# Three attention layers in one kernel: the first layer's step plan re-ordered, and the cross layer's softmax denominators taken from one sum per pair of heads

## The reference, cut to what matters

```python
# first layer (L0): 20 heads of 8, two softmaxes on one set of queries
out = softmax(q k_text^T) v_text + softmax(q k_ip^T) v_ip      # 77 text keys, 435 ip keys
x = x + out @ Wo.T + bo
# a1: self-attention, 20 heads of 64, on n = layer_norm(x)
x = x + attention(n, n)
# a2: cross-attention, 20 heads of 64, keys and values from the context (512 keys)
x = x + attention(layer_norm(x), context)
x = x + feed_forward(layer_norm(x))
```

## Time and profile before

| | |
|---|---|
| median of 3 runs | 1611.23 us (1607.58 to 1615.48) |
| the profiled execution | 1616.8 us, of it 1615.0 us span |
| PE busy | 1536.3 us, 95% |
| VectorE / ScalarE / GpSimd busy | 64% / 48% / 29% |
| chain that ended last | PE 80%, VectorE 7%, ScalarE 6%, issue 6% |
| mean granted TensorE clock | 0.967 of full |

### The profile page before, as it was taken

The page is one execution under the profiler, slowest core; times in us unless marked ns, Lnnn a source line. Parts: engine busy times, 40 slices in busy tenths (PEclk is TensorE's granted clock), DMA queues, the critical chain, the costliest instruction groups (busy, mean ns, idle before and its releaser), DMA issues.

```text
span 1615.0 us, 41102 instructions
## 1 busy us (share of the span) xinstructions
PE 1536.3 (95%) x18128; PEld 1208.6 (75%) x18128; DVE 1028.1 (64%) x1410; ACT 776.1 (48%) x1061; POOL 465.9 (29%) x414
## 2 busy tenths in 40 slices
PE   7999999878999999999899999999999999999988
PEld 5566666546888887888778878888787878777788
DVE  6777777763776776766556555565655555565466
ACT  3666666654444454455344444444444444443323
POOL 4332333220222232334322332232322332232300
PEclk7989999968999999999999999999999999999999
DMA  5322232100000100000110000000000020000000
GB/s 149 94 58 59 58 132 63 43 1 22 2 2 2 58 35 2 6 2 18 37 48 2 2 28 2 28 2 28 2 28 2 1 71 2 1 2 2 2 13 21
DMA packets 26780, 45.54 MB, mean 28 GB/s; under 512 B 7344, under 2 KB 15472, under 8 KB 26224
## 3 DMA queue, kind: packets, MB, share of 16 engines
q1 hardware_dynamic: 26608, 42.96, 8.8%
HBM read 29.51 MB, written 1.31 MB: 19 GB/s over the span
## 4 chain that ended last, share of the span: by engine, by line
PE 80%; DVE 7%; ACT 6%; issue 6%; DMA 1%; POOL 0%; SPq 0%; ACTq 0%; POOLq 0%; DVEq 0%
PE a_pj L949 7%; PE a_pj L961 7%; PE l_px L1530 5%; PE a_pv L983 5%; PE a_px L983 4%; PE a_pj L495 4%; PE l_pscore L1453 3%; PE a_px L536 3%; PE a_pst L914 3%; PE a_pscore L893 3%; PE a_pv L522 3%; PE l_pst L1468 2%; PE a_px L999 2%; PE a_pj L504 2%; PE a_pst L920 2%
## 5 line engine op out<-in xcount | busy, mean ns | idle before, releaser
L1204 POOL TENSOR_TENSOR a_key_sum<-a_probs 128x512 f32<-128x512 f32 x160 | 209.4, 1313 | 449.4 <-ACT a_probs L1052 449.4
L1131 DVE TENSOR_REDUCE a_negmax<-a_pscore 128x2 f32<-128x1024 f32 x160 | 195.6, 1222 | 105.0 <-PE a_pscore L893 104.6
L1052 ACT ACTIVATE a_probs<-a_pst 128x1024 f32<-128x1024 f32 x160 | 164.1, 1026 | 168.3 <-PE a_pst L920 167.7
L1762 DVE TENSOR_REDUCE l_negmax<-l_pscore 128x2 f32<-128x154 f32 x320 | 203.5, 685 | 48.3 <-PE l_pscore L1453 47.6
L1647 ACT ACTIVATE l_probs<-l_pst 128x1024 f32<-128x1024 f32 x160 | 164.0, 1025 | 98.6 <-PE l_pst L1468 98.3
L736 POOL TENSOR_TENSOR a_key_sum<-a_probs 128x1024 f32<-128x1024 f32 x40 | 96.3, 2408 | 246.4 <-ACT a_probs L582 246.4
L655 DVE TENSOR_REDUCE a_negmax<-a_pscore 128x4 f32<-128x1024 f32 x80 | 97.6, 1220 | 54.4 <-PE a_pscore L453 54.3
L1145 DVE RECIPROCAL a_recip<-a_pv 128x256 f32<-128x256 f32 x40 | 70.3, 1757 | 88.9 <-PE a_pv L989 88.9
L961 PE MATMUL a_pj<-a_wv_hi,a_ct 128*128 128x256 f32 x640 | 111.2, 285 | 0.0
L582 ACT ACTIVATE a_probs<-a_pst 128x1024 f32<-128x1024 f32 x80 | 81.9, 1024 | 40.2 <-PE a_pst L479 36.3
L914 PE MATMUL a_pst<-a_qh,a_kh 64*128 64x256 f32 x640 | 96.7, 293 | 2.5 <-ACT a_probs L1052 1.5
(11 more groups left out here) (219 smaller groups left out, 3504.0 us busy)
## 6 DMA issues: line engine op xcount, KB each, us to landing
l_ct<-in_ctx_t SPq DMA_DIRECT2D x8, 512.0 KB, 4.3
l_k_stack<-l_k_hi SPq DMA_DIRECT2D x64, 64.0 KB, 2.1
a_ct<-in_ctx_t SPq DMA_DIRECT2D x8, 512.0 KB, 4.6
a_ct<-in_ctx_t SPq DMA_DIRECT2D x16, 256.0 KB, 5.1
l_q_stack<-l_q_hi SPq DMA_DIRECT2D x80, 32.0 KB, 1.9
l_x<-in_x_t SPq DMA_DIRECT2D x8, 256.0 KB, 4.2
l_k_stack<-l_k_lo SPq DMA_DIRECT2D x32, 64.0 KB, 2.1
a_raw_wq<-in_a_wq SPq DMA_DIRECT2D x2, 960.0 KB, 4.6
```

What stands on the lines that cost most here:

```text
L1052: nc.scalar.activation(probs[:, 2 * i:2 * i + 2, 2 * n:2 * n + 2, :], pst[:].rearrange("p h (k q) -> p h k q", k=2), ACT.Exp, scale=SCALE) ...
L1131: nc.vector.tensor_reduce(to, pscore[:], AX.X, ALU.max, negate=True).then_inc(max_done, 1)
L1204: nc.gpsimd.tensor_tensor(key_sums[n][:, two], probs[:, two, 2 * n, :], probs[:, two, 2 * n + 1, :], ALU.add).then_inc(sum_ready, 1)
L1762: last = nc.vector.tensor_reduce(to[:, :, k], pscores[s % 2][:, :, keys], AX.X, ALU.max, negate=True)
```

## The change

1. **Cross layer**: POOL makes three of the four additions; DVE adds, behind its fourth maximum of the step, the sums of heads 0-1, then the last pair of key tiles of heads 2-3, then the sums of heads 2-3, and only then the low keys. PE multiplies one sum instead of two.
2. **First layer, plan**: "out" moves from part 3 into part 1 of u = 2 and into another PSUM bank (`pj`, written by place 0 as well), with DVE adding it in part 1; the first value projection moves from u = 3 to u = 2, and the others up by one place. `norm` moves from step 37 to 35.
3. **First layer, start**: the marks are loaded ahead of the context; DVE writes those of buffer 0 before it takes the low keys and those of buffer 1 later; DVE, not POOL, rounds stack 0; PE waits for one value tile, ahead of its second score.
4. **Opening of a1**: it starts 3 steps earlier, in step 30, and its copies stand one by one between the parts of a step, `wv` in three pieces in step 36. The split weights lie in tensors of their own (`SplitMatrix`), and each is loaded by two DMAs.
5. All SBUF addresses (`AT`) are new.

```diff
-    PLAN = {0: ("ip", "text"), 1: ("q", "rest"), 2: (None, None), 3: ("v0", "v1"), 4: ("v2", "v3")}
+    PLAN = {0: ("ip", "text"), 1: ("q", "rest"), 2: (None, "v0"), 3: ("v1", "v2"), 4: ("v3", None)}
...
-        if t == ALL - 3:
+        if t == ALL - 5:
             return ("norm", place)
         b, u = divmod(t, GROUPS)
+        if u == 2 and place == 0 and 0 <= b - 2 < B - 1:
+            return ("out", b - 2)
...
-        OPEN, LOAD, FF_OPEN = S0 - 7, 24, S2 - 5
+        OPEN, LOAD, FF_OPEN = S0 - 10, 24, S2 - 5
...
-            for n in range(2):
-                pe.wait_ge(sum_ready, 4 * e + 2 * n + 2)
-                for t in range(4):
-                    last = mm(pv[t * 32:(t + 1) * 32, SQ:2 * SQ], ones[:], key_sums[n][:, t, :],
-                              start=n == 0, stop=n == 1)
+            for i in range(2):
+                pe.wait_ge(sum_ready, 2 * e + i + 1)
+                for t in (2 * i, 2 * i + 1):
+                    last = mm(pv[t * 32:(t + 1) * 32, SQ:2 * SQ], ones[:], key_sums[0][:, t, :], start=True, stop=True)
...
+        def sum_halves(e):
+
+
+            add = nc.vector.tensor_tensor
+            dve.wait_ge(half_summed, 3 * e + 3)
+            add(key_sums[0][:, 0:2], key_sums[0][:, 0:2], key_sums[1][:, 0:2], ALU.add).then_inc(sum_ready, 1)
+            dve.wait_ge(exp_done, SLOTS * (e + 1))
+            add(key_sums[1][:, 2:4], probs[:, 2:4, 2, :], probs[:, 2:4, 3, :], ALU.add).then_inc(last_summed, 1)
+            dve.wait_ge(last_summed, e + 1)
+            add(key_sums[0][:, 2:4], key_sums[0][:, 2:4], key_sums[1][:, 2:4], ALU.add).then_inc(sum_ready, 1)
...
+            if s == 3 and here(d - 2):
+                sum_halves(d - 2)
             if s == 3 and here(d):
                 low_keys(d)
...
                 for i in range(2):
                     two = slice(2 * i, 2 * i + 2)
+                    if (n, i) == (1, 1):
+                        continue
```

More of the change, by code:

```diff
@@ L596, in copy_values, with opening @@
             copy(v[:, d % RING], pj[:, :, 0:STEP_COLS]).then_inc(v_copied, 1)
[L598 to L605, removed]
-            if k == 3:
+        def opening(k, s):
+            if (k, s) == (0, 0):
+                act.wait_ge(loaded[0], 32)
+                copy(wq.hi[:], wq.raw[:]).then_inc(w_hi, 1)
+            if (k, s) == (0, 2):
+                copy(wq.rest[:], wq.raw_rest[:]).then_inc(w_hi, 1)
+            if (k, s) == (2, 0):
+                act.wait_ge(wq_done, 4)
+                act.wait_ge(loaded[1], 32)
+                copy(wk.hi[:], wk.raw[:]).then_inc(w_hi, 1)
+            if (k, s) == (2, 2):
+                copy(wk.rest[:], wk.raw_rest[:]).then_inc(w_hi, 1)
+            if (k, s) == (4, 0):
+                ln.act_xhat(act, 0, (0,))
+            if (k, s) == (4, 2):
+                ln.act_xhat(act, 0, (1,))
+            if (k, s) == (6, 0):
+                act.wait_ge(*ahead["normed"])
+                ln.act_hi(act, 0, nts[0])
+            if (k, s) == (6, 1):
+                act.wait_ge(wk_done, 4)
@@ L607, in opening @@
                 for moved in ahead["moved"]:
                     act.wait_ge(*moved)
[L609 to L621 removed]
+                act.wait_ge(loaded[2], 32)
@@ new lines, in opening @@
+                copy(wv.hi[:, 0], wv.raw[:, 0]).then_inc(w_hi, 1)
+            if (k, s) == (6, 2):
+                copy(wv.hi[:, 1], wv.raw[:, 1]).then_inc(w_hi, 1)
+            if (k, s) == (6, 3):
+                copy(wv.rest[:], wv.raw_rest[:]).then_inc(w_hi, 1)
+            if k == 8 and s in (0, 2):
+                i = s // 2
+                act.wait_ge(*ahead["rounded"])
+                nc.scalar.activation(sel[:, i, :], ident[:, i:i + 1].broadcast_to([P, P]), ACT.Identity,
+                                     bias=ident[:, D1 + i:D1 + i + 1]).then_inc(sel_set, 1)
@@ L1375, in stack_queries @@
             sp.wait_ge(q_low, m + 1)
-            wait(sp, rounded, GROUPS * (m - 1) + u + 1)
+            wait_rounded(sp, GROUPS * (m - 1) + u)
             main = u < GROUPS - 1
@@ L1448, in score @@
             if s == 0:
-                pe.wait_ge(rounded, g + 1)
+                wait_rounded(pe, g)
+            if g == 0 and s == 1:
+                pe.wait_ge(first_read, 1)
             wait(pe, max_done, 4 * g + s - 1)
@@ L1512, in project @@
                     last = next_norm.turn(g, pj[:, i * SQ:(i + 1) * SQ])
+                last.then_inc(pj_ready, 1)
+                return
+            if what == "out":
+                pe.wait_ge(px_read, px_uses["s2", m] + 1)
+                for qt in range(QT):
+                    last = output(qt, pj)
                 last.then_inc(pj_ready, 1)
@@ L1594, in part @@
             if s == 3:
-                if finished(t) and finished(t)[0] == "out":
-                    wait(pe, px_read, px_uses[finished(t)])
-                    for qt in range(QT):
-                        last = output(qt, px)
-                    last.then_inc(px_ready, 1)
-                elif finished(t):
+                if finished(t):
                     finish(*finished(t))
@@ L1790, in take, with mark @@
         def take(what, b):
+            if what == "out":
+                dve.wait_ge(pj_ready, pj_uses[what, b] + 1)
+                add_output(b, pj[:, 0:QT * C]).then_inc(pj_read, 1)
+                return
             dve.wait_ge(px_ready, px_uses[what, b] + 1)
-            if what == "out":
-                add_output(b, px[:, 0:QT * C]).then_inc(px_read, 1)
-                return
             if what == "s0" and b:
-                dve.wait_ge(px_ready, px_uses["out", b - 1] + 1)
+                dve.wait_ge(pj_ready, pj_uses["out", b - 1] + 1)
             multiply(int(what[1]), b, px).then_inc(px_read, 1)
+        def mark(v):
+            nc.vector.memset(v[:, 1:KT, :, ROWS // 2:ROWS // 2 + 1], 1.0)
+            for k in range(2):
+                cols = slice(k * ROWS // 2, k * ROWS // 2 + 1)
+                last = nc.vector.tensor_scalar(v[:, 0, :, cols], v[:, 0, :, cols], marks[:, k:k + 1], None, ALU.add)
+            last.then_inc(v_marked, 1)
         def multiply_last():
@@ L1834, in part @@
                 low_rest(t // GROUPS + 2)
+            if s == 1 and projected(t, 0) and projected(t, 0)[0] == "out":
+                take(*projected(t, 0))
             if s == 2 and here(t - 1):
@@ L1889, in begin @@
             split_inputs(1)
-            for g in range(GROUPS):
+            for g in range(1, GROUPS):
                 round_stack(g)
@@ L1911, in narrow_attention_layer @@
                 max_done=(max_done, 4 * ALL), exp_done=(exp_done, 4 * ALL), finished=(last_done, 4),
-                moved=[(stacked[u], MOVES[u] * B) for u in range(GROUPS)])
+                moved=[(stacked[u], MOVES[u] * B) for u in range(GROUPS)],
+                rounded=(rounded, ALL - 1), normed=(pj_read, pj_uses["norm", 1] + 1))
 def feed_forward_layer(nc, ctx, places, tag, xs, ident, dram, out, ahead):
```

158 lines of the change are left out of this document (79 added, 79 removed), and 47 rows, old and new, of the table AT.

## The result

| | median us | runs | ratio to before | 95% interval |
|---|---|---|---|---|
| before, beside the first series | 1620.7 | 20 | | |
| changed kernel | 1606.41 | 20 | 0.994 | 0.9912 to 0.9968 |
| before, beside the second series | 1626.2 | 17 | | |
| changed kernel again | 1607.53 | 12 | 0.9903 | 0.987 to 0.9936 |

The kernel before has a median of 1621 to 1626 us when it is run more often; the 1611.23 of the prediction was the median of three. So ratios count here: forecast 0.9825, measured 0.994 and 0.9903, a gain of 10 to 16 us instead of 28. A ratio leaves out the executions that are over 1.5% above the fastest of their kernel, so it isn't the quotient of the two medians, which would be gains of 14 and 19 us. The forecast of 1583 and the range up to 1601 both missed the 1606. Taken as a ratio, the range ends at 0.9937: the first series lies just outside it, the second inside.

A forecast was written before the change was run, and what follows sets the result against it. PE, 95% busy, was taken as the bound, with first-layer idle gaps sometimes bringing a lower clock. Gains of 7 + 5 + 5.7 + 10 + 0 = 27.7 us took 1616.8 to 1589, the median 1611.23 to 1583; range 1563 to 1601.

The forecast's parts named there:

- Part 4, the opening: End of first layer: spreading a1's weight copies and subtractions over earlier steps gains 10 us, bounds 0 and 20.
- The steps 35 to 40: End of first layer: these steps would take 9 us each, 45 in all, instead of 54.85.
- Part 2, the plan: First layer: closing PE's gaps gains 5 us, and less time at the lower clock behind steps 7 and 12 gains 5.7.
- 0.3 us for the spread product in u = 4: First layer, u = 4: charge per batch because part 3 keeps only the spread reciprocals, 1.7 us in all.
- the 1.81 us of the earlier trace: Cross layer: VectorE additions this slow beside GpSimd's work would make the kernel slower, median about 1670; rival at 4%.
- Part 1, the cross layer: Cross layer: 19.6 us saved, less 8.4 for stalls and 4 for lower clock, gives 7 us gained, between 20 and nothing.
- The saving: Cross layer: half the denominators' 16 instructions go, 0.49 us a step over 40 steps, 19.6 us of PE.
- The stall of the norm steps: Cross layer, 7 steps in which a norm starts: PE stalls 1.2 us each because GpSimd begins its additions late, 8.4 us.
- The 4 us for a lower clock behind it: Cross layer: about one in five of the 7 norm-step stalls is followed by the lower clock; bounds 0 and 21.
- The start: First layer's start, marks loaded first and first score not waiting for values: 0, bounds 1 lost and 3 gained.
- the second, the first layer gives little: Rival: lower clock comes anyway and gaps only move; parts 2 to 4 give some 8 us, median about 1597; 22%.
- the first, the cross layer gives more: Rival: additions hidden everywhere, norm steps too; the cross layer's part gives 19 us, median about 1569; 15%.

The follow-up runs named there:

- c4: The kernel before with the opening of a1 alone as in the change (norm turned in step 35): 1620.98 us, ratio 1.0028.
- f2: d5 with ScalarE's copy of wk's high part waiting for the low parts of wq again, as in the change: 1593.68 us, ratio 0.9877.
- f3: d5 with the plan and start of the first layer as before; opening, cross layer and other edits stay: 1583.61 us, ratio 0.9834.
- c6: The kernel before with the cross layer's part alone, GpSimd's three sums ahead of its reciprocal deviation where a norm starts: 1601.5 us, ratio 0.9857.
- c3: The kernel before with the plan and start of the first layer as changed, opening of a1 as before: 1611.7 us, ratio 0.9954.
- c1: The kernel before with the cross layer's part of the change alone: 1609.46 us, ratio 0.9913.
- d5: Changed kernel with low rest moved, wk copy released by last input split, GpSimd's cross-layer sums first, a1's first norm statistics earlier: 0.9722, again 0.9754.
- d1: The changed kernel with VectorE's low rest moved from part 1 to the end of part 3 of u = 4: 1602.38 us, ratio 0.9914.
- d4: Changed kernel with low rest moved, wk copy released by last input split, and GpSimd's cross-layer sums ahead of its reciprocal deviation: 1585.76 us, ratio 0.9812.
- c2: The changed kernel with the cross layer's part taken back, leaving only the first layer's parts: 1619.12 us, ratio 0.9963.

## Why the prediction was wrong, step by step

- **Part 4, the opening, is where it failed.** The step reads: "ScalarE's copies of wq and wk and VectorE's subtractions for them fall into steps 30 to 33, where the two have room." They had room; GpSimd was left out of the sum. The diff gives the copy of wk a wait for `wq_done`, and GpSimd's two subtractions of 1.5 us each for it stand behind its splitting and rounding for the first layer. I named what is queued behind neither that wait nor the later one for GpSimd's shift. Predicted 10 us gained; measured alone (c4), 1.0028, with nothing at all inside the interval and the 10 us outside it; put back alone (f2), the wait costs 20 us. What the opening is worth with both waits mended is open: in f3 (old plan) a1 begins at 354.9 us against 371.0, but that is one profile, and the ratios of f3 and c6, which differ by the opening as mended, are 0.9834 and 0.9857, 4 us apart and within each other's intervals.
- **The steps 35 to 40** did become shorter, 50.27 us where I had 45 and before had 54.85.
- **Part 2, the plan, came out near its net size** when alone: 10.9 us at the start of a1 against 10.7, 0.9954 by the ratio (7.5 us), 10 to 13 in f3. No wait of PE stood in step 12 any more, and the clock was 1.00 where it should be. Some of the agreement is luck: in c3's profile the low rest was never slow, and in f3's the clock held without the plan. Missing was the low rest: I had charged 0.3 us for the spread product in u = 4, and in the changed kernel the batches in which the collision struck lost 4.4 to 5.4 us each. I had read the 1.81 us of the earlier trace rows as a risk for the new additions, and not looked for other pairs of the same kind that the change brings into line.
- **Part 1, the cross layer, was too low**: 7 forecast, 14 by the ratio of c1. The mechanism held, the additions at 0.68 to 0.69 us, eight instructions in 0.61, no stall in ordinary steps. Three terms were mis-sized. The saving is 0.43 us a step, 17.2 in 40 steps and not 19.6, since the start-to-start time fell from 0.98 to 0.55 and not to half. The stall of the norm steps was 5.5 us and not 8.4. The 4 us for a lower clock behind it didn't come: 1000 to 1200 us ran at 1.00. 17.2 - 5.5 is 11.7, and the rows of the layer show 8.2 to 11.4; where the rest of the 14 lies is left open below.
- **The start** at nothing was not contradicted: step 5 stands at 62.86 us against 62.85, though the first score came 1.3 us earlier.
- **The rival that came** was the second, the first layer gives little, at 22%, together with the first, the cross layer gives more. Its reason, "the gaps only move", fits the profiles. I gave it too little, since I had counted the gaps that the change removes and not the waits that it adds.

## What to carry to other kernels

List every wait that a change adds, and for each the whole queue of the engine that must signal it, the idle one too: here an engine at 26% busy held up PE. In this kernel a gap of a microsecond in front of TensorE cost itself or, in one profile, some sixteen; removing one of several such gaps may show nothing, so test by putting each back alone into a kernel that has none. And where two instructions on VectorE and GpSimd are released by the same event, put one of them behind the other's end: in before the low rest began 1.57 us behind GpSimd's 2.37 us subtraction and still took 1.07.

## What the runs showed of the hardware

- **One after the other.** Of VectorE's 32x256 subtraction with two inputs in SBUF and GpSimd's 128x1024 one, the one that starts some 0.05 us later is the one that is longer: 0.42 us becomes 2.59, or 2.37 becomes 2.59. Both together take 2.64 us from the first start to the last end either way; what changes is who waits. The Trainium skill (GPSIMD Engine Reference, Specifications) has the two engines share their SBUF interfaces, with contention for VectorE instructions of two SBUF inputs; the trace agrees.
- **The same gap, two outcomes.** d5 was profiled twice. PE waits 1.11 us for an exponential in step 7 both times, and these are the windows behind it:
```profile
74.00:110.00 36.00, 35.88 (x344) 23.10 (x344) 29.37 (x47) 25.36 (x37) 12.53 (x17) 1.00 0.25 66
```
```profile
74.00:110.00 36.00, 35.39 (x202) 21.44 (x203) 19.59 (x31) 15.54 (x21) 8.68 (x13) 0.52 0.24 65
```
PE was 98% busy in the second, and it still ran at 0.52 for 36 us. Between steps 6 and 14 the second execution falls 15.9 us behind the first, and a1 begins 23.5 us later, for the same program. The second profile is of one of the longer runs of d5, but d1 and f2 show the same stretch. The Trainium skill (TensorE: Matmul & The Clock Gate, Part 1) says, of the matmuls at a kernel's start, that the gate's observation runs free of the program, so that one kernel can fare differently from run to run. These two executions differ in that way, though in the middle of the kernel. Why it then stays low for so long under full load isn't settled by any run here. It makes a single profile of this first layer a poor measure, and is why c6, profiled with a1 beginning at 402.5, still has one of the better medians.
- **Left open.** The stretch behind the last low queries of the cross layer took 122.5 us before and 117.4 to 117.5 in c1, c6 and d4, but also 118.6 to 120.8 in c2 to c4, which don't have the cross part; so some 1 to 5 us of its gain lie there, and which, isn't settled. Nor is it shown why steps 35 to 40 kept 50 us in the changed kernel.
